# v's bias as a three-row matmul, the denominators' mask product and the expert-mix addition on GpSimd

## What is computed

```python
x = x + att(_ln_c(x))          # attention over the 16 images at each (row, column)
    # zn = layernorm(z) * ln_w + ln_b;  q, k, v, g from zn @ W
    # att = softmax(q.k / 4, axis=images);  o = (att @ v) * sigmoid(g);  out = o @ Wo + bo
t = t + ffn(_ln_t(t))          # 8 experts, the two best mixed by their router weights
    # expert_out = x @ expert_w + expert_b;  out = sum_k top_p[k] * expert_out[top_i[k]]
x = x + conv(_ln_c(x))         # expand, running mean along rows, sigmoid gate, contract
    # state_primary * sigmoid(ema(state_gating)) @ W_con + b_con
```

## Time and profile before

| | us |
|---|---|
| median of 3 runs | 3073.49 |
| lowest and highest | 3064.63, 3075.29 |
| the profiled execution | 3058.97 |
| its span on the core | 3057.2 |

### The profile page before, as it was taken

The page is one execution under the profiler, slowest core; times in us unless marked ns, Lnnn a source line. Parts: engine busy times, 40 slices in busy tenths (PEclk is TensorE's granted clock), DMA queues, the critical chain, the costliest instruction groups (busy, mean ns, idle before and its releaser), DMA issues. The chain is left out here.

```text
span 3057.2 us, 108311 instructions
## 1 busy us (share of the span) xinstructions
PE 2587.4 (85%) x36971; PEld 1910.3 (62%) x36971; DVE 2555.4 (84%) x9012; ACT 1991.3 (65%) x3590; POOL 2181.0 (71%) x2967
## 2 busy tenths in 40 slices
PE   2888888888888988888888888888888888888378
PEld 1666666666666666666666666666666666666258
DVE  1798888888888888888888888888888888888536
ACT  3666677667767666767677667777776776765240
POOL 2677778777777777777778777878777777776320
PEclk9887889788988788888879788988888898887579
DMA  0011010101101001011010101011010101010379
GB/s 17 9 20 20 16 20 18 19 17 19 18 18 19 18 18 19 18 18 20 18 19 18 19 16 20 17 19 19 18 19 18 20 18 18 18 18 15 121 238 375
DMA packets 263152, 106.90 MB, mean 35 GB/s; under 512 B 251281, under 2 KB 253876, under 8 KB 258997
## 3 DMA queue, kind: packets, MB, share of 16 engines
q1 hardware_dynamic: 262085, 101.81, 13.7%
q10 hardware_dynamic: 1008, 4.29, 0.4%
HBM read 55.56 MB, written 50.33 MB: 35 GB/s over the span
## 5 line engine op out<-in xcount | busy, mean ns | idle before, releaser
L472 ACT ACTIVATE kT<-s_bank,b_k,block_of 128x512 f32<-128x512 f32 x1024 | 748.9, 771 | 3.6 <-PE s_bank L609 0.3
L640 PE MATMUL s_bank<-kT,qT 128*32 128x128 f32 x8192 | 394.6, 372 | 189.8 <-issue 189.7
L640 PEld LDWEIGHTS s_bank<-kT,qT 128*32 128x32 f32 x8192 | 348.0, 152 | 229.5 <-issue 227.2
L489 ACT ACTIVATE qT<-shared,b_qkg 128x256 f32<-128x256 f32 x256 | 107.5, 470 | 411.0 <-PE shared L609 411.0
L811 DVE TENSOR_REDUCE mixed<-yg 128x256 f32<-128x2048 f32 x128 | 288.5, 2254 | 0.2
L687 PEld LDWEIGHTS o_bank<-w_o,ogT 128*128 128x128 f32 x2048 | 248.0, 193 | 21.2 <-DVE ogT L839 12.0
L414 POOL TENSOR_TENSOR probs<-weights,own_den 128x1024 f32<-128x1024 f32 x128 | 251.7, 1966 | 1.8 <-DVE own_den L857 1.8
L387 POOL TENSOR_TENSOR split_ffn<-norm_ffn,split_ffn 128x256 fp32r<-128x256 f32 x128 | 93.4, 730 | 220.6 <-ACT split_ffn L464 220.6
L687 PE MATMUL o_bank<-w_o,ogT 128*128 128x64 f32 x2048 | 246.6, 274 | 2.9 <-DVE ogT L839 2.7
L658 PEld LDWEIGHTS o_bank<-probsT,v_sb 32*32 32x32 f32 x16384 | 169.8, 106 | 64.5 <-issue 58.9
L387 POOL TENSOR_TENSOR split_att<-norm_att,split_att 128x256 fp32r<-128x256 f32 x128 | 93.7, 732 | 147.4 <-ACT split_att L464 147.4
(11 more groups left out here) (214 smaller groups left out, 7543.6 us busy)
## 6 DMA issues: line engine op xcount, KB each, us to landing
x_in<-in_x SPq DMA_DIRECT2D x1024, 16.0 KB, 1.7
x_scratch<-x SPq DMA_DIRECT2D x1024, 16.0 KB, 1.4
normalized_x_scratch<-norm_pick SPq DMA_DIRECT2D x1024, 16.0 KB, 1.5
xa<-normalized_x_scratch SPq DMA_DIRECT2D x8, 1024.0 KB, 8.2
xc<-normalized_x_scratch SPq DMA_DIRECT2D x8, 1024.0 KB, 12.4
out_x<-xc SPq DMA_DIRECT2D x16, 512.0 KB, 4.8
xc<-x_scratch SPq DMA_DIRECT2D x4, 1024.0 KB, 9.4
xb<-x_scratch SPq DMA_DIRECT2D x4, 1024.0 KB, 17.1
```

Source lines behind the costliest of these rows:

```text
L472: ins = s.activation(kT[:, h, :], bk("k")[:], ACT.Identity, bias=b_k[:, h:h + 1], scale=block_of[:, h:h + 1])
L640: ins = t_.matmul(s_bank[g * 32:(g + 1) * 32, 0, t * P:(t + 1) * P], qT[z][:, c, tok:tok + 32], kT[:, :, tok + c * N:tok + (c + 1) * N], s ...
```

## The change

Three edits, and no other work is reordered.

1. v's bias. GpSimd's addition (L406) goes, with its semaphore; the attention values now wait for ScalarE's copy of v. In its place a matmul of three ones with `bv3` (v's bias, four times side by side, as three bfloat16 rows) begins the accumulation in v's bank, and the four matmuls of v add to it. The rows are made once, before the first slot, by four small VectorE instructions more, one of them uncounted, and a second DMA behind the one for `bias3`. Their scratch lies in `yg`.
2. The denominators. VectorE's product with the mask becomes GpSimd's, directly ahead of the product that uses it, with a semaphore (`own_denominators`) between the two.
3. The addition x2 = mixed + x1. VectorE's instruction becomes one of GpSimd, between the second part of the ffn split and the attention's norm. It waits for `mixed`.

```diff
@@ gpsimd, step @@
                     if runs(i, q, 4):
                         second_part("ffn", i, q, 4)
+                    if runs(i, q, 5):
+
+                        z = par(q, 5)
+                        pool.wait_ge(s_mixed, at(i, q, 5))
+                        g.tensor_tensor(x2[z][:], mixed[:], x1[z][:], ALU.add).then_inc(s_x2, 1)
                     if runs(i, q, 0):
 
                         normalize("att", x_in[q], 1.0 + 1e-5, 1e-6 * 1e-5, i, q, 0, "att_t")
...
-                    if runs(i, q, 1):
-
-                        z = par(q, 1)
-                        pool.wait_ge(drained["v"], at(i, q, 1))
-                        g.tensor_tensor(v_sb[z][:], v_sb[z][:], bv_rows[:].unsqueeze(1).broadcast_to([P, QT, HC]),
-                                        ALU.add).then_inc(s_v, 1)
...
                         pool.wait_ge(s_rden, at(i, q, 2))
                         wait(pool, s_probsT, at(i, q, 3))
+                        g.tensor_tensor(own_den[:], ssum[:].unsqueeze(2).broadcast_to([P, 32, 2]),
+                                        odd_even[:].unsqueeze(1).broadcast_to([P, 32, 2]), ALU.mult).then_inc(s_own, 1)
+                        pool.wait_ge(s_own, at(i, q, 2))
@@ tensor, step @@
-                        wait_apart(pe, (s_probsT, at(i, q, 3)), (s_v, at(i, q, 3)), (s_og, at(i, q, 4)),
+                        wait_apart(pe, (s_probsT, at(i, q, 3)), (drained["v"], at(i, q, 3)), (s_og, at(i, q, 4)),
...
                         bank_free(pe, i, q, "v")
+                        t_.matmul(bk("v")[:], ones3[:], bv3[:], start=True, stop=False)
                         for t in range(QT):
-                            ins = t_.matmul(bk("v")[:, tile(t)], zT[z1][:, tile(t)].bitcast(F32), w_scaled[:, 3, :])
+                            ins = t_.matmul(bk("v")[:, tile(t)], zT[z1][:, tile(t)].bitcast(F32), w_scaled[:, 3, :],
+                                            start=False, stop=(t == QT - 1))
@@ vector, step @@
                         dve.wait_ge(drained["y3"], at(i, q, 5))
+                        wait(dve, s_x2, at(i, q, 6))
                         v.tensor_reduce(mixed[:], yg[:],
                                         AX.X, ALU.add).then_inc(s_mixed, 1)
...
-                        dve.wait_ge(s_mixed, at(i, q, 5))
-
-                        wait(dve, s_x2bc, at(i, q, 7))
-                        v.tensor_tensor(x2[z][:], mixed[:], x1[z][:], ALU.add).then_inc(s_x2, 1)
                         dve.wait_ge(s_x2, at(i, q, 5))
                         stats("conv", x2[z], i, q, 5)
...
                         dve.wait_ge(s_exp, at(i, q, 2))
-                        ch = Chain(dve, s_sums, 2, i, q, 2)
+                        wait(dve, s_own, at(i, q, 3))
+                        ch = Chain(dve, s_sums, 1, i, q, 2)
                         ch.link(v.tensor_reduce(ssum[:], weights[:], AX.X, ALU.add))
                         ch.join()
-                        ch.link(v.reciprocal(ssum[:], ssum[:]))
-                        ch.join()
                         ch.end()
-                        v.tensor_tensor(own_den[:], ssum[:].unsqueeze(2).broadcast_to([P, 32, 2]),
-                                        odd_even[:].unsqueeze(1).broadcast_to([P, 32, 2]), ALU.mult).then_inc(s_rden, 1)
+                        v.reciprocal(ssum[:], ssum[:]).then_inc(s_rden, 1)
```

More of the change, by code:

```diff
@@ L109, in build @@
             bias_row = cb("bias_row", [1, NE * D])
-            bias_rest = cb("bias_rest", [1, NE * D])
             bias_parts = cb("bias_parts", [1, 3, NE * D], BF16)
@@ L113, in build @@
             bv_terms, bv_ones = cb("bv_terms", [D, HC]), cb("bv_ones", [D, P])
-            bv_rows = cb("bv_rows", [P, HC])
+            bv3 = cb("bv3", [3, QT * HC], BF16)
             ones3 = cb("ones3", [3, P], BF16)
@@ L158, in build @@
             yg = cb("yg", [P, QT, D, NE])
+            scratch_row = yg[0:1].rearrange("o t d e -> o (t d e)")
+            bias_rest, bv_row, bv_rest = scratch_row[:, 0:512], scratch_row[:, 512:640], scratch_row[:, 640:768]
+            bv_parts = scratch_row[:, 768:1536].bitcast(BF16).rearrange("o (k t c) -> o k t c", k=3, t=QT)
             mixed = cb("mixed", [P, QT, D])
@@ L183, in build @@
             s_top, s_diff, s_ratio, s_gates = sem("top_chain"), sem("top_diff"), sem("top_ratio"), sem("gates_done")
-            s_sums, s_v = sem("exp_summed"), sem("values_biased")
+            s_sums, s_own = sem("exp_summed"), sem("own_denominators")
             s_mixed, s_x2, s_x2bc = sem("experts_mixed"), sem("x2_done"), sem("x2_bc_done")
@@ L191, in build @@
             N_POOL_SETUP = 12
-            N_DVE_SETUP = 11
+            N_DVE_SETUP = 14
             def at(i, q, lag, n=1, more=0):
@@ L306, in _ @@
                 sp.dma_start(bias3[:], bias_parts[:]).then_inc(s_bias3, 16)
+                sp.dma_start(bv3[:], bv_parts[:]).then_inc(s_bias3, 16)
                 def step(i, q):
@@ L451, in _ @@
                 s.copy(b_qkg[:], shared[1][:, 0:3]).then_inc(s_act_setup, 1)
-                s.copy(bv_rows[:], shared[1][:, P:2 * P]).then_inc(s_act_setup, 1)
+                s.copy(bv_row[:], shared[1][0:1, P:2 * P]).then_inc(s_act_setup, 1)
                 s.copy(w_expand_hi[:], shared[0][:, 0:P]).then_inc(s_act_setup, 1)
@@ L588, in _ @@
                 pe.wait_ge(s_dve_setup, N_DVE_SETUP)
-                pe.wait_ge(s_bias3, 16)
+                pe.wait_ge(s_bias3, 32)
                 def transposed(name, kind, i, q, lag):
@@ L749, in _ @@
                 v.tensor_copy(w_expert_hi[:].rearrange("d (c e) -> d c e", e=NE), w_expert[:].rearrange("d e c -> d c e"))
+                v.tensor_copy(bv_parts[:, 0], bv_row[:].unsqueeze(1).broadcast_to([1, QT, HC]))
                 v.tensor_copy(bias_parts[:, 0, :].rearrange("o (c e) -> o c e", e=NE),
@@ L765, in _ @@
                                       by_channel(bias_parts[:, 0, :]), ALU.subtract))
+                setup(v.tensor_tensor(bv_rest[:], bv_row[:], bv_parts[:, 0, 0], ALU.subtract))
                 setup_join()
+                spread = bv_rest[:].unsqueeze(1).broadcast_to([1, QT, HC])
                 setup(v.tensor_copy(bias_parts[:, 1, :], bias_rest[:]))
+                setup(v.tensor_copy(bv_parts[:, 1], spread))
                 setup_join()
                 setup(v.tensor_tensor(bias_parts[:, 2, :], bias_rest[:], bias_parts[:, 1, :], ALU.subtract))
+                setup(v.tensor_tensor(bv_parts[:, 2], spread, bv_parts[:, 1], ALU.subtract))
                 setup_join()
```

## The result

The changed kernel takes 3206.8 us (3201.1 to 3212.5) against 3074.4 us of the kernel before beside it: 1.042 times as long, 95% interval 1.036 to 1.048. The forecast was 3082, at most 3128: wrong, and on the slower side.

A forecast was written before the change was run, and what follows sets the result against it. Bound to x1: VectorE in plain slots, PE in scan slots. Plain 20.2 plus scan 22.8 makes 43.0 us a pair, 43.3 with clock; 64 pairs +7, setup +2, giving 3068 profiled, 3082 median; 8 in 10: 3035 to 3128.

The forecast's parts named there:

- The chain of edit 3: From `mixed` through GpSimd's addition, norm, `split_att` and `tT`: `scan_out` at 6.68 us at the earliest, x1 at 10.53, every slot.
- Edit 1: v's bias to PE: 0.15 us gain left in plain slots; matmul 0.4 us, on the path only in low-clock scan slots.
- the stall: VectorE's gating held up by GpSimd's bias addition and `split_conv`: 2.38 us against 0.85, so 1.5 us goes.
- Edit 2: Mask product to GpSimd: nothing gained on VectorE, costs nothing, or at worst up to 0.3 us a slot.
- It costs nothing while that holds: Holds while the transposition reads `probs` over 3 us later and `split_ffn` has waits covering a delay under 1.5 us.
- The tails: Time from x1 to the next slot's start of `mixed`: 9.7 us in plain slots, 12.24 in scan slots.
- The clock: Rival: PE's idle ahead of `scan_out` slows scores; 3119 us in half the pairs (20%), 3177 in all (8%).
- its two groups: Plain slots with `scan_out` at 6.35 or later, then full-clock scores; at 5.6 or earlier, then partly low-clock scores.
- 0.35 was allowed for the clock: Added per pair for one pair in four with a low-clock stage, 24.20 against 22.82 us.

The follow-up runs named there:

- f1: Kernel before plus one line: GpSimd waits for `mixed` ahead of the attention's norm, no work moved; 3129.4 us, 1.014.
- e3: Changed kernel with GpSimd's addition x2 = mixed + x1 placed behind the attention's norm, ahead of its second part; 3029.6 us, 0.987 of the kernel before.
- e2: Kernel before with only the addition moved to GpSimd, ahead of the attention's norm; 3198.8 us, 1.043.
- h1: Kernel before with only v's bias moved to the matmul on PE; 3032.4 us, 0.985.
- h2: Changed kernel with the mask product back on VectorE, the addition left where the change has it; 3142.6 us, 1.024 of the kernel before.
- e4: Changed kernel with v's bias matmul issued five times, the first four overwritten; 3148.4 us, 1.026 of the kernel before.
- g1: Changed kernel with the addition behind the attention's norm and the mask product back on VectorE; 2981.0 us, 0.971 of the kernel before.
- f2: Changed kernel with the addition behind the attention's norm and `x_bo` ahead of the second part of the convolution's split; 3149.5 us, 1.020 of the kernel before.

## Why the prediction was wrong

By its own steps:

- **The chain of edit 3: right.** 6.68 and 10.53 in plain slots, 5.73 for `split_att`, 0.727 us for the addition; the statistics wait for nothing. f1 and e3 show that the wait's place makes it. In scan slots it is 6.93 and 10.92 on average, not 6.68 and 10.53: 0.39 us a pair short.
- **Edit 1: right in the sum, wrong in what it is worth.** The gating takes 0.96 us where 2.38 stood, and the matmul 0.39. But the step weighed the stall against x1 of the kernel before (0.15 us left). Beside edit 3 the stall would have set x1 at 12.02 (e2). Alone edit 1 gives 1.5% (h1), beside edit 3 1.9% (e2 to h2). What a stall is worth depends on what sets x1 in the new kernel, not in the old one.
- **Edit 2: the step that failed.** "It costs nothing while that holds" rested on the transposition and on `split_ffn`. The durations were right (`own_den` 0.29 us, `probs` from 11.79 to 13.72), but the step didn't follow GpSimd's queue to the next instruction, `x_bo`, which starts 13.68 after the slot's start, beside `lgm`, and frees `x_in` for its load. Its worst case was 0.3 us a slot, 38 us; it cost 64 (h2), of which `lgm` and the load are 0.81 us a pair, 52 us, and the rest comes with the long slots. That VectorE gains nothing from it was right here. The Trainium skill, SBUF — State Buffer (SBUF: two separate sides), has the rule: one of the two holds the port pair for a whole instruction, and the other blocks. The trace agrees (0.77 beside 0.73). The prediction used this rule for v's bias and the gating, where it took a stall away, and not for what the edit moved into its reach.
- **The tails: mis-sized.** 9.7 and 12.24 were put down, 10.80 and 12.71 are the means, 1.57 us a pair. h2's 9.99 and 12.24 share this out: 1.28 goes with the mask product (0.86 if slots of 25 us or more, whose tails are 13.18 to 14.31, are left out on both sides), 0.29 is left. The two terms were read from single slots: in the kernel before the means are 10.18 and 12.63, 0.87 a pair above them. So the forecast counted on a fall, by the gates, which did go from 285 to 202 ns, and by scores at full clock, which came in less than half of the scan slots.
- **The clock: the right rival, at the wrong place.** The forecast held that a late `scan_out` gives full-clock scores. Not so: the scores take over 2.6 us, so are at least partly at the low clock, in 25 of 48 scan slots (33 of 50 before: the 25 that the prediction counted and 8 more, at 3.43 to 3.46 us, behind plain slots with `scan_out` at 6.22 to 6.24, which its two groups left out). But that costs nothing that shows: x1 of scan slots is at 10.84 on average behind these scores and at 11.01 behind the others, and `scan_out` waits for `tT` in 34 of the 48. What costs is the idle that this wait puts just ahead of `scan_out` and the attention output. All ten slots of 25 us or more follow scores at full clock. The rival named this idle and let it slow the scores; its worst case was 3177. The ten slots of 25 us or more are 1.05 us a pair above the medians of their kinds (20.92 and 23.23), where 0.35 was allowed for the clock. e4 took the six plain ones away and gained 58 us.

Together: plain x1 +0.54, plain tail +1.10, scan x1 +0.39, scan tail +0.47 make 2.50 on 43.0 us a pair; 0.3 was allowed, so 2.2 x 64 = 141 us, against the 133 by which the profiled execution exceeds 3068. Against the means of the kernel before (x1 at 10.34 and 10.03), the chain alone moves x1 by 0.69 us a pair, 44 us; the forecast let its lower tails hide this.

Why v's bias and the mask product hinder each other isn't settled. One part may be that both edits remove the same stall: `own_den` on VectorE takes 519 ns in the earlier trace rows, 248 with v's bias alone off GpSimd (h1), and in h2 less than the 292 ns that it takes on GpSimd:

```profile
L864 DVE TENSOR_TENSOR own_den<-ssum,odd_even 128x64 f32<-128x64 f32 x81 | 18.2, 225 | 2.8
```

So beside edit 1 there is less left for edit 2 to save. More is in the groups: with v's bias on PE and the addition behind the norm, the mask product brings `lgm` from 179 to 248 ns, VectorE's wait for `x_in` from 1.6 to 11.8 us in all, and low-clock scores in scan slots from 17 of 52 to 25 of 51. This doesn't add up to the 1.65% between g1 and e3. The rest would lie in how slots of different clock follow each other, and no run took that apart.

## What to carry to other kernels

In a queue that runs in order, an instruction costs by what it waits for and who stands behind it: place moved work behind the first instruction that others wait for, even if it could run sooner. Follow a delay through the whole queue, up to the point where it meets another engine or a load, not just to the reader of the delayed result. And measure edits apart and together: here two of the three, one of them placed elsewhere, are 3% faster than before, and all three as written 4% slower.

## What was unexpected of the hardware

- The clock can fall and rise in a fixed pattern. In h1, plain slots come in turn with 18.8 and 22.1 us from 419 to 2552 us. Two slots in stretches, the first plain, the second scan; and the scores after each, of which the second belong to the slow plain slot:

```profile
1613.70:1632.56 18.86, 16.07 (x241) 11.09 (x233) 17.85 (x72) 14.15 (x26) 14.53 (x22) 1.00 0.09 17
1632.56:1654.35 21.79, 18.43 (x305) 13.74 (x308) 19.50 (x73) 16.38 (x30) 16.69 (x23) 0.93 0.12 22
```
```profile
1632.47 1.95 PE L638 MATMUL s_bank<-kT,qT 128*32 128x128 f32 x64 [1.47 <-issue]
...
1652.99 3.64 PE L638 MATMUL s_bank<-kT,qT 128*32 128x128 f32 x64 [2.44 <-issue]
```

  The idle just ahead of the scores does not tell the level: in h1, 51 scores between 400 and 2600 us follow 2.44 us of idle, and 26 of them take 1.95 us, 25 take 3.64. In the change 36 follow 1.47 us, and 17 take 1.95 us, 19 over 3 us.
- The same level reached in two ways has two prices: 0.911 by four filling matmuls in a wait gained 58 us, 0.913 by the same four without a wait lost 98 us against 0.858.
- A VectorE instruction over 32 elements a partition takes 0.77 us when it starts with a GpSimd addition of 0.73, and 0.18 alone; the same happens to a copy of 8 elements with a single input beside `probs` (1.14 us in f2, 0.17 in the change's slot above).
